# A two-layer decoder in fp32: logits inside cross attention, a token-major linear attention, early expert weights, and y stored by scatter

## The reference, cut to what matters

```
x = x + L0_attn(layernorm(x))            # softmax attention over exterior products ("lines"), causal
x = x + L0_xattn(layernorm(x), ctx)      # 16 heads of 16, 375 keys
x = x + L0_ffn(layernorm(x))             # 8 experts 256 -> 1024 -> 256, relu, top 2, softmax over the two
x = x + L1_attn(layernorm(x))            # linear attention, 8 heads of 32 (below)
x = x + L1_xattn(layernorm(x), ctx)
x = x + L1_ffn(layernorm(x))             # 8 experts, top 1, weight = its softmax probability
```

```
kv = einsum('bshd,bshe->bhde', k, v);  ksum = k.sum(axis=1);  vsum = v.sum(axis=1)
num = einsum('bshd,bhde->bshe', q, kv) * scale + vsum
den = einsum('bshd,bhd->bsh', q, ksum) * scale + seq_len
o = num / den + lepe_conv(v)             # depthwise, 5 taps over tokens, with a bias
out = (o * (x @ Wg.T)) @ Wo.T
```

## Time and profile before

| | us |
|---|---|
| median of 3 timed runs | 1753.49 (1752.35 to 1757.32) |
| the profiled execution's own time | 1737.61 |
| its span, first to last instruction | 1735.5 |

### The profile page before, as it was taken

How to read it: one execution, slowest core, us unless ns; L and a number is a source line. 1 busy time by engine, 2 the same in 40 slices (tenths; PEclk the granted TensorE clock), 3 DMA queues, 4 the chain that set the end, 5 groups by cost and what they waited for, 6 DMA issues and landing times. The chain is left out here.

```text
span 1735.5 us, 35382 instructions
## 1 busy us (share of the span) xinstructions
PE 1419.8 (82%) x13764; PEld 1099.0 (63%) x13764; DVE 754.8 (43%) x1813; ACT 540.6 (31%) x1222; POOL 414.6 (24%) x502
## 2 busy tenths in 40 slices
PE   5887689999987499999807666658999998759996
PEld 2555456677765499999605555535776766549994
DVE  4555345555522422222345666644555652132224
ACT  2655134555531122222102111102555553112220
POOL 5665200000001344444351111120000000124443
PEclk8999779999995699999858888756999997659997
DMA  6000011111101499999410000001111110139993
GB/s 205 2 2 2 13 28 29 31 33 33 31 6 43 164 328 325 329 322 329 143 56 1 0 0 0 0 13 24 33 35 29 36 28 6 43 128 336 325 323 118
DMA packets 62474, 170.45 MB, mean 98 GB/s; under 512 B 18715, under 2 KB 43659, under 8 KB 48012
## 3 DMA queue, kind: packets, MB, share of 16 engines
q0 software_dynamic: 21120, 130.53, 21.1%
q1 hardware_dynamic: 41228, 38.14, 8.0%
HBM read 139.37 MB, written 12.85 MB: 88 GB/s over the span
## 5 line engine op out<-in xcount | busy, mean ns | idle before, releaser
L912 DVE TENSOR_REDUCE xa_mx<-xa_ps_s 112x2 f32<-112x750 f32 x256 | 241.0, 941 | 245.5 <-PE xa_ps_s L657 242.1
L663 PEld LDWEIGHTS xa_ps_p<-xa_qT,xa_kT 32*125 32x125 f32 x3072 | 197.0, 188 | 112.9 <-ACT xa_p L836 78.7
L663 PE MATMUL xa_ps_p<-xa_qT,xa_kT 32*125 32x112 f32 x3072 | 239.6, 287 | 31.9 <-DVE xa_mx L912 11.1
L836 ACT ACTIVATE xa_p<-xa_ps_p 125x672 f32<-125x672 f32 x256 | 187.0, 730 | 239.6 <-PE xa_ps_p L663 239.6
L657 PE MATMUL xa_ps_s<-xa_kT,xa_qT 32*112 32x375 f32 x1024 | 244.3, 555 | 11.5 <-DVE xa_mx L912 7.7
L1516 PEld LDWEIGHTS ex_ps_h<-ex_xT,ex_w 128*128 128x128 f32 x1792 | 213.3, 195 | 10.4 <-DMA ex_w<-in_experts0a,ex_now 3.9
L1516 PE MATMUL ex_ps_h<-ex_xT,ex_w 128*128 128x128 f32 x1792 | 213.9, 279 | 6.8 <-DMA ex_w<-in_experts0a,ex_now 3.5
L1527 PE MATMUL ex_ps_y<-ex_w,ex_hT 128*128 128x256 f32 x896 | 202.7, 379 | 0.0
L1527 PEld LDWEIGHTS ex_ps_y<-ex_w,ex_hT 128*128 128x128 f32 x896 | 165.9, 190 | 20.2
L1550 ACT ACTIVATE ex_hT<-ex_ps_h,ex_w 128x128 f32<-128x128 f32 x224 | 70.0, 363 | 274.9 <-PE ex_ps_h L1516 268.7
L1562 DVE TENSOR_SCALAR ex_hT<-ex_ps_h,ex_w 128x128 f32<-128x128 f32 x224 | 68.3, 347 | 173.3 <-PE ex_ps_h L1516 172.1
(11 more groups left out here) (271 smaller groups left out, 2224.2 us busy)
## 6 DMA issues: line engine op xcount, KB each, us to landing
xa_kT<-xa_kU SPq DMA_DIRECT2D x128, 93.8 KB
ys<-ex_y SPq DMA_DIRECT2D x56, 128.0 KB
xa_qT<-xa_qU SPq DMA_DIRECT2D x64, 56.0 KB
xn<-rt_xn SPq DMA_DIRECT2D x8, 448.0 KB
cT<-in_ctxT SPq DMA_DIRECT2D x4, 750.0 KB, 8.3
xa_qT<-xa_nmT SPq DMA_DIRECT2D x128, 1.8 KB
x<-in_x SPq DMA_DIRECT2D x4, 448.0 KB, 5.6
out_x<-x SPq DMA_DIRECT2D x16, 112.0 KB
```

The costliest lines, as they stand in the source:

```text
L663: return pe.matmul(bp[0:CT, i, c * S:(c + 1) * S], kT[r:r + 32, b % RB, n, c * CT:(c + 1) * CT], qT[r:r + 32, b % RB, n, :], start=True, s ...
L836: act.activation(p[slot % 4][:, :, :], bp[0:CT, :, 0:NC3 * S], ACT.Exp).then_inc(exped, 1)
L912: dve.tensor_reduce(mx[:, b % 2, j:j + 2, n], bsc[0:S, :, 0:CL], AX, ALU.max).then_inc(maxed, 1)
```

## The change

In `cross_attention` the start is in another order, and each row's second norm, store and logits follow its `finish` inside the loop, which runs one row longer (VectorE's two). Persistent tiles hold the logits and routing's constant tables, which GpSimd now makes in layer 0's `cross_attention`. `route` loses its loop and fetches the weights of tiles 0 and 1. `experts` stores y by an indirect DMA to the tokens' places, and `combine` reads y with direct DMAs. `linear_attention` is written anew, token-major. Some contractions run over their two halves in the other order, and the shift LIFT is 0.49 instead of 0.5 times ln 2.

```diff
 def cross_attention ... @block.tensor
+            def row_turn(b):
+                pe.wait_ge(x2_normed, b + 1)
+                pe.wait_ge(k_copied, min(2 * (b + 5), 2 * NB))
+                reused(pe, lg_set, b)
+                for c in range(2):
+                    last = pe.transpose(bk[:, c * S:(c + 1) * S], x2[:, b % 4, c * P:(c + 1) * P], g.ident[0:S, 0:S])
+            def logits(b):
+                pe.wait_ge(x2_t, b + 1)
+                for c in range(2):
+                    last = pe.matmul(bk[0:S, 2 * P:2 * P + NE], x2T[:, c, :], g.wr[:, layer, c, :], start=(c == 0), stop=(c == 1))
...
-            idle_products(bp[:, 0, 0:P], 10)
-            pe.wait_ge(set_v, 2 - layer)
-            pe.wait_ge(v_set, 1)
...
-            for t in range(-3, NB + 1):
+            keys(0, 0)
+            for t in range(-3, NB + 2):
...
                     if t == -2:
-                        idle_products(bp[:, 0, 0:P], 10)
+                        bias_rows()
+                        idle_products(bp[:, 0, 0:P], 5 + 4 * layer)
...
+                if on(t - 2):
+                    row_turn(t - 2)
                 round_of(t, 7)
...
                     out_product(t - 1)
+                if on(t - 2):
+                    logits(t - 2)
 ... @block.vector
+            dve.memset(zeros[:, :, :], 0.0).then_inc(zeros_set, 1)
+            dve.memset(qT[:, 0, :, :], 0.0).then_inc(zeros_set, 1)
...
+                    if slot == 0 and on(t - 3):
+                        row_logits(t - 3)
...
+                    if slot == 3 and on(t - 2):
+                        second_norm(t - 2)
...
                         normed_row(t + 3)
+                        if t == -3:
+                            first_tiles()
 ... @block.gpsimd
-            pool.memset(zeros[:, :, :], 0.0).then_inc(zeros_set, 1)
-            pool.memset(qT[:, :, :, :], 0.0).then_inc(zeros_set, 1)
-            for u in range(RB):
+            pool.memset(qT[:, 1:RB, :, :], 0.0).then_inc(qT_set, 1)
+            for u in range(1, RB):
                 pool.memset(kT[:, u], 1.0).then_inc(ones_set, 1)
...
+                    pool.tensor_scalar(g.rstd[:, b:b + 1], g.mv[:, b, 1:2], LN_EPS, None, ALU.add).then_inc(x2_scaled, 1)
+                    pool.wait_ge(x2_scaled, 2 * b + 1)
+                    pool.tensor_tensor(g.rstd[:, b:b + 1], g.rstd[:, b:b + 1], g.nhalf[:, 0:1], ALU.pow).then_inc(x2_scaled, 1)
```

```diff
 def linear_attention ... @block.tensor, the whole loop
+            for t in range(NB + 2):
+                if on(t):
+                    queries_keys(t)          # 2 products, 512 columns
+                if on(t - 1):
+                    keys_values(t - 1)       # 2 x 136 columns: v and two groups of 4 columns of ones
+                    q_turn(t - 1)
+                if on(t):
+                    values_gates(t)          # 2 products, 512 columns
+                if on(t - 2):
+                    o_turn(t - 2)            # waits for gated
+                if on(t - 1):
+                    convolution(t - 1)       # 10 products of 128 columns, the taps on diagonals
+                    numerators(t - 1)        # per half 136 + 128 columns (ones times v: vsum)
+                if on(t + 1):
+                    x_turn(t + 1)
+                if on(t):
+                    v_turn(t)
+                if on(t - 2):
+                    out_product(t - 2)
 ... @block.vector
+            for t in range(NB + 3):
+                if on(t - 2):
+                    divide(t - 2)            # 3 operations of 8 columns, 1 of 256
+                if on(t - 3):
+                    add_out(t - 3)
+                if on(t):
+                    rope(t)                  # 512 + 2 x 256 columns
+                if on(t - 2):
+                    add_conv(t - 2)
+                    gate_row(t - 2)
+                if on(t - 1):
+                    mask_kv(t - 1)           # 272 columns, both parts of the denominators masked
+                if on(t + 1):
+                    normed_row(t + 1)
+                if on(t - 3):
+                    row_stats(t - 3)
 ... @block.gpsimd
+            for t in range(NB + 2):
+                if on(t - 2):
+                    lift_row(t - 2)          # o1 + the convolution's bias
+                if on(t):
+                    rope_sum(t)
```

```diff
 def route
+            fetch(0)
+            pool.wait_ge(ew.second_found, 1)
+            pool.tensor_copy(ew.rows[:, 1:2], ew.second[:, :]).then_inc(ew.row_set, 1)
+            pool.wait_ge(ew.row_set, 2)
+            fetch(1)
...
-            for b in range(NB):
-                link(dve.tensor_tensor(cum[:, b + 1, :], cum[:, b, :], tot[:, b, :], ALU.add))
+            for n in range(4):
+                old, new, d = sums[n % 2], sums[1 - n % 2], 1 << n
+                link(dve.tensor_tensor(new[:, NB // 2:, :], old[:, NB // 2:, :], old[:, NB // 2 - d:NB // 2 + NB - d, :], ALU.add))
...
+            link(dve.scalar_tensor_tensor(wrf[:, :], bt[:, NTILE:2 * NTILE], 0.0, spare[:, :], ALU.is_equal, ALU.mult))
+            link(dve.tensor_tensor(wrf[:, :], wrf[:, :], turns[:, :], ALU.add))
+            link(dve.tensor_copy(trow[:, 0:NTILE], wrf[:, :]))
 def experts ... @block.gpsimd
+            def scatter(m, slot):
+                pool.wait_ge(y_copied, m + 1)
+                pool.wait_ge(aimed, m + 1)
+                aim(m + 1, (slot + 1) % NW)
+                pool.indirect_dma_start(y_dram, bass.IndirectOffsetOnAxis(ap=to[:, slot, :], axis=0), y[:, slot % 2, :], None) \
+                    .then_inc(stored[slot % 2], 16)
...
                     gather(m + 2, (u + 2) % NW)
+                if not isinstance(m, int) or m > 0:
+                    scatter(m - 1, (u - 1) % NW)
 def combine ... @block.sync
+            for n in range(4):
+                for k in range(top):
+                    rows = y_dram[(1 + k * NB + 4 * n) * S:(5 + k * NB + 4 * n) * S]
+                    sp.dma_start(yg[:, 4 * n:4 * n + 4, k, :], rows.rearrange("(b t) d -> t b d", t=S)).then_inc(y_in[n], 16)
```

787 lines of the change are left out of this document (449 added, 338 removed).

## The result

| | before | after |
|---|---|---|
| median of 4 timed runs, us | 1755.4 (1752.35 to 1759.05) | 1573.8 (1559.76 to 1578.51) |
| ratio | | 0.8945, 95% interval 0.8896 to 0.8994 |
| profiled execution, us (span) | 1737.6 (1735.5) | 1559.8 (1558.0) |

The forecast was 1583 us in a range of 1547 to 1625. The profiled execution is the fastest of the four.

A forecast was written before the change was run, and what follows sets the result against it. TensorE was taken to bound cross attention's main part and the experts (859 us), with chains elsewhere. Terms summed to -170.6 us: profiled 1737.6 to 1567.0, plus 15.9 gives 1583 us, range 1547 to 1625.

The forecast's parts named there:

- the logits: Logits leave `route`: of 41.6 us per layer before the choice, 5.5 remain; -72 us in both layers.
- `route`: Routing's own chain: fewer dependent additions and links, against some added links; net -3 us over both layers.
- the early fetch: Weights fetched during `route`, so the experts' first products wait less; DMA engines idle there, nothing delayed; -5.5 us.
- Linear attention: Rewritten stage: 10.1 us a row, with one wait at `o_turn` for the gated row; -67.3 us.
- The two norms: VectorE's norm in linear attention, 0.98 us beside `rope_sum`, 0.40 alone; offered as agreeing with the exclusion rule.
- The rival of the low clock: Linear attention's clock stays near 0.8, rows take 12.1 us: +28, 1611 us; chance 0.15.
- Added to a row of cross attention: Second norm, transposes and logits' products per row cost 0.5 us in 28 rows, mostly in round 7: +14 us.
- not what it says: Rival: the logits' extra waits, bank shared with keys, pace the cross rounds; 32 x 2 us, 1647 us; chance 0.03.
- Start of cross attention: Reordered start brings the first score, taken to wait for spread queries, earlier: -9.9 and -4.4, together -14.3 us.
- The store of y: In the experts, y's store moves from SP to GpSimd: hidden in 56 tiles, last scatter waited for; +2.6 us.
- Combine: SP's direct reads replace gathers, VectorE 1.2 us a row: -22.5 in layer 0, -2.6 in layer 1, together -25.1 us.
- The carried difference of 15.9 us: Median of timed runs lies 15.9 us above the profiled execution; carried from before to the forecast, 1567.0 to 1583 us.

The follow-up runs named there:

- the added wait: The changed kernel, but GpSimd's `rope_sum` also waits for VectorE's `gate_row` of two rows before: row 8.73 us (9.57), ratio 0.8825 to the kernel before.

## Why the prediction was right

**What bounds the kernel; the logits, `route` and the early fetch.** Right in mechanism and size: -73.5 for -72, -3.0 for -3, -5.0 for -5.5. Only "nothing is delayed by it", said of the early fetch, looked at the DMA engines alone and not at GpSimd's drain, which ends last in layer 1. The power of one column took 0.57 us, where I took 1.0 for it and its scale (0.87 with the gap).

**Linear attention.** The row was 8.9 us of products and one wait at `o_turn`; measured 9.57 with 0.69 of wait, forecast 10.1 with 1.0 to 1.2. The mechanism of the wait was the forecast's, and the added wait showed it: `gate_row` beside `rope_sum` is what costs. By the Trainium skill (SBUF — State Buffer, Who interferes with whom) a VectorE instruction with two SBUF inputs and a GpSimd instruction that reads SBUF shut each other out whole. The runs agree, 1.26 beside 0.42 us with `rope_sum` as long either way, and again 0.83 beside 0.40 in combine, where the forecast had not used it. The two norms that the forecast gave as agreeing are not this case: they have one tensor as input and two operands of one column. The rest of the 11 us that the stage fell below the forecast is 14 x 0.5 = 7.4 us and a shorter fill: the first rows came 4.7 and 8.1 us apart, for 8 and 11. The rival of the low clock did not come: 0.98.

**Added to a row of cross attention.** +14 was forecast as 28 rows at 0.5, measured +12.3, but the step was wrong by its parts. Steady rows cost 0.85 each, 0.28 in round 7 (0.45 forecast) and 0.54 in round 0, which I had costed at nothing because VectorE idles 0.42 us there. I looked at VectorE's slack and not at what stands behind the added operation: the bank that the keys write next. The rival "not what it says" named the bank, at the wrong price of 2 us. Without the clock these rows would have missed by more: 0.85 in 28 rows is 24 us. What hid the difference was the clock, which is luck: before, layer 1's main part had low stretches from 1437 to 1468, in which its last two rows took 23.8 and 17.8 us where layer 0's took 16.5 and 14.0. After, only the row before the last of layer 1 was long, 21.6. The lead-ins nearly cancel, 34.2 to 29.8 in layer 1 and 31.6 to 36.7 in layer 0.

**Start of cross attention.** -11.4 for -14.3. I took the spread queries as the last thing that the first score waits for. In the changed kernel it waits for none: in both layers it starts as TensorE's own idle products end. In layer 0 the whole start ran at 0.50 of the clock, and the constant row with the router's bias and the idle products took TensorE 5.6 us, from 193.3 on. In the kernel with the old linear attention, where the clock had risen, they took 3.7 us, and there the score waited 0.41 us for the queries.

**The store of y.** In the tiles nothing, as forecast; at the end of the stage 12.1 us where I had 2.6, above my bound of 6. The failed step is "the last scatter is waited for, some 1.3 us later than the direct store": the landing is early enough, but GpSimd's drain comes behind it, and the scatter moved GpSimd's last DMA from three tiles before the end to the end. The Trainium skill (DMA: Bandwidth & Descriptors, SWDGE vs HWDGE vs iDMA) says that plain transfers go to SP or ScalarE and irregular ones to GpSimd. The price in a tile that the forecast drew from it did not come: the scatter's issue takes GpSimd 0.99 us, and the tiles stayed at 7.24 us but for the one long one.

**Combine.** -31.1 for -25.1. VectorE's row was 1.55 us beside GpSimd and 1.12 after, 1.2 forecast; that GpSimd's additions "run beside" at no cost was wrong by 3.2 us, and the waits I had added (2 us) did not come. In layer 1 sixteen gathers at 1.24 us a row gave way to 0.73 us a row; I had taken the output's stores for the limit there.

The sum missed by 6.9 us in the profiled executions (-177.5 for -170.6), linear attention and combine 17.5 to the good, the experts' ends 9.5 and the starts 2.9 to the bad, so it is as near as it is because the misses cancel. The carried difference of 15.9 us between profile and median came out as 14.0; nothing in the forecast said why it should stay.

## What to carry to other kernels

Before an added operation is costed at nothing, ask what shares its bank or tile and who waits for that: here 0.15 us of VectorE in an idle gap cost 0.54 us a row, until it was put ahead of a 0.94 us neighbour. Two engines' operations that slow each other in the trace can be kept apart with one wait where the later has slack; that was worth 11 us in the stage. An indirect DMA that becomes the last thing GpSimd does before a barrier costs its drain too, several microseconds that no busy row shows.

## What the runs showed of the hardware

GpSimd's drain at the end of a block took 3.1 to 3.5 us (35 tiles) and 6.5 to 6.9 us (21 tiles) with a scatter as its last DMA, the same whether that DMA was the last or the last but one tile's, 14.1 to 18.3 us where the experts' weights were the last, 15.2 to 18.0 us behind the gathers of the old combine, 8.3 to 9.7 us behind the early fetch in `route`, and 2.0 to 2.3 us behind plain additions in combine; what sets the length stays open.

With three idle products of 128 columns a round both lead-ins ran at the upper clock, in one profile; with one a round layer 0's did in some profiles and not in others, and layer 1's never all through. That the products keep the clock up is likely and not shown. A stretch in which TensorE was busy for 35.7 of 36.7 us stayed at the lower level. Why the clock falls near the end of cross attention in some runs, which costs up to 6 us in the row before the last and 9 in the last, was not found out.
